# Unread TensorE products in half step 13 and inside the dt product of half step 22 of a Mamba block with a feed-forward tail

## The chip, the core and the metric

The kernel runs on one core of one Trainium2 chip. The metric is the device time of one execution in microseconds (us); less is better. The core's engines run side by side and meet at semaphores only: TensorE (PE; its weight loads are listed as PEld), VectorE (DVE), ScalarE (ACT), GpSimd (POOL) and SyncE (SP, which issues most of the DMAs). TensorE has two clock levels here, 1.2 and 2.4 GHz; the profile gives the granted clock as a share of the upper one, 0.50 or 1.00.

## What is computed

x has the shape 2 x 2048 x 256. All is float32. Cut to what matters:

```python
# both parts: x = x + layernorm(part(layernorm(x)))
def mamba(x):                                  # d_inner 512, state 16, conv width 4
    h = x * rsqrt(mean(x * x) + EPS) * norm_w
    u, z = split(h @ in_proj_w.T)
    uc = silu(conv_b + sum(pad(u)[k:] * conv_w[:, k] for k in range(4)))
    dt, B, C = split(uc @ x_proj_w.T)
    dt = softplus(dt @ dt_proj_w.T + dt_proj_b)          # the dt product
    h_t = exp(dt * A) * h_prev + dt * B * uc             # one scan per state
    y = sum_n(C * h_t) + uc * D
    return (y * silu(z)) @ out_proj_w.T + x
def ffn(x):                                    # hidden 1024, ternary weights
    h = silu(x @ w1.T * s1) * (x @ w2.T * s2)
    h = gelu(h @ h1.T * sh1)
    h = gelu(h @ h2.T * sh2)
    return h @ w3.T * s3
```

## The kernel before

The 4096 tokens are cut into 16 chunks of 256. The program is written by hand for each engine, with semaphores, and is cut in the same way on all of them: `body(c, par, ...)` is called once for each chunk c and runs through 32 half steps (`hs` 0 to 31), two for each of the 16 states. In the body of chunk c four pieces of work are interleaved: the scan of chunk c itself, the head of chunk c+1 (norm, in_proj, convolution, x_proj, dt product), the tail of chunk c-1 (the Mamba output, w1, w2 and h1 of the feed-forward part) and the end of chunk c-2 (h2, w3 and the last norm). Chunks 2 to 13 stand in a loop over pairs; bodies 2 to 14 have all four pieces, and the body of chunk 15 has no head.

The order on an engine is the order in which the code is written. On TensorE it is, within a half step: `turn` (four transposes of 128x128 that turn half of the scan's result S of the state before, L753), the piece of `end_step`, the piece of `tail_step`, the piece of `head_step`. An engine waits at a semaphore with all that stands behind it.

The pieces that matter here, by half step of the body:
- hs 10 to 13: the head's four in_proj products, L717, out `hP`. The two of hs 12 and 13 wait for ACT's copies of z out of `hP` (L1210), since they write over the same banks. ACT's copies of u (L1214) and the convolution follow.
- hs 14: `last_product` (w3), 32 products in L857 and L858, reading `Ghi` and `Glo`.
- hs 15 and 16: the first two quarters of w1 (`branch`, L729 and L730), each after the hs's turn. POOL's product `S<-X,Bs` (L567) of a later state needs the slot of S that the turn frees; ACT's `load_B` (L1160) in hs 16 waits for that product's step (L570), and behind it on ACT stand `dA` (L1134) and the copies of w1's results (L1298), which the next w1 products wait for.
- hs 22: two transposes of `xdbl` (L785), then the dt product in two halves, L793 (q = 0 and q = 1, two products each); the second waits for ACT's copy of `CT` (L1233).
- hs 24 to 31: the h1 layer, one tile of 16 products in each half step (L729, L730, in `Ghi`, `Glo` and `w_h`).

`keep_warm` (L796 to L801) makes products whose result nobody reads: ident by ident, 128x128, into a PSUM bank of the ring `fP` before its next use, after waiting for the bank's last reader. Before the change it is called in hs 22 and in hs 23 of the tail, six products each; in the profile one such product is two MATMUL records.

Of the kernel before, what the change touches and what calls it, by code (L numbers as in the profile page):

```python
# [25 lines left out]
P = 128  # L26
# [26 lines left out]
def build(nc, x, in_proj, x_proj, dt_proj, out_proj, w1, w2, h1, h2, w3, cols, w3_s, out):  # L53
# [22 lines left out]
    with ctx:  # L76
# [24 lines left out]
        ident = sb("ident", [P, P])  # L101
# [606 lines left out]
        def _(pe):  # L708
# [45 lines left out]
                                      ident[:, :])  # L754
                mm.then_inc(turn_pe.sem, 1)

            def head_step(h, hp, hs):
                if hs == 8:
                    pe.wait_ge(head_act.sem, head_act.at(h, "hn"))
                    pe.wait_ge(head_vec.sem, head_vec.at(h - 1, "delta"))  # L760
                    for k in range(KM):
                        for t in range(TT):
                            mm = pe.transpose(hP[0][:, k, t * P:(t + 1) * P], hn[:, t, k * P:(k + 1) * P],
                                              ident[:, :])
                    mm.then_inc(head_pe.sem, 1)
                if 10 <= hs < 14:
                    q = hs - 10
                    if q == 0:
                        pe.wait_ge(head_act.sem, head_act.at(h, "hT"))
                    elif q >= 2:  # L770

                        pe.wait_ge(head_act.sem, head_act.at(h, ("z0", "z1")[q - 2]))
                    for d in range(2):
                        m = (2 * q + d + DT) % (2 * DT)
                        mm = products(hP[(q + 1) % 2][:, d, :], lambda k: w_in[:, k, m * P:(m + 1) * P],
                                      lambda k: hT[:, k, :], KM)
                    mm.then_inc(head_pe.sem, 1)
                if hs == 20:
                    pe.wait_ge(head_act.sem, head_act.at(h, "silu1"))
                    products(hP[1][0:XC, 0, :], lambda k: w_x[:, k, :], lambda k: uc[hp][:, k, :],  # L780
                             DT).then_inc(head_pe.sem, 1)
                if hs == 22:
                    pe.wait_ge(head_act.sem, head_act.at(h, "dtx"))
                    for t in range(TT):
                        mm = pe.transpose(hP[1][:, 1, t * XC:(t + 1) * XC], xdbl[:, t * P:(t + 1) * P],  # L785
                                          ident[0:XC, 0:XC])
                    mm.then_inc(head_pe.sem, 1)
                    for q in range(2):
                        if q == 1:
                            pe.wait_ge(head_act.sem, head_act.at(h, "ct"))  # L790
                        for d in range(2):
                            m = 2 * q + d
                            mm = pe.matmul(hP[q][:, d, :], w_dt[:, m * P:(m + 1) * P], dtx, start=True, stop=True)  # L793
                        mm.then_inc(head_pe.sem, 1)

            def keep_warm(f, fp, count):  # L796

                steps, chunk, name = last_reader(f + 1, "h1_0")
                pe.wait_ge(steps.sem, steps.at(chunk, name))
                for _ in range(count):  # L800
                    pe.matmul(ring(1 - fp, "h1_0")[:, 0, 0:P], ident[:, :], ident[:, :], start=True, stop=True)  # L801

            def branch(f, fp, which, i, stream):

# [64 lines left out]
            def tail_step(f, fp, hs):  # L869
                if hs == 2:  # L870
                    for i in range(2):
                        steps, chunk, name = last_reader(f + 1, f"yT{i}")
                        pe.wait_ge(steps.sem, steps.at(chunk, name))
                        for t in range(TT):
                            pe.wait_ge(acc_vec.sem, acc_vec.at(f, f"y{t}_{N - 1}"))
                            for d in range(2):
                                mm = pe.transpose(ring(1 - fp, f"yT{i}")[:, d, t * P:(t + 1) * P],
                                                  acc[:, t, (2 * i + d) * P:(2 * i + d + 1) * P], ident[:, :])
                        mm.then_inc(tail_pe.sem, 1)
                if hs == 3:  # L880
                    pe.wait_ge(tail_vec.sem, tail_vec.at(f, "yz1"))
                    steps, chunk, name = last_reader(f + 1, "out")
                    pe.wait_ge(steps.sem, steps.at(chunk, name))
                    for t in range(TT):
                        mm = products(ring(1 - fp, "out")[:, t, :], lambda k: z[fp][:, k, t * P:(t + 1) * P],
                                      lambda k: w_out[:, k, :], DT)
                    mm.then_inc(tail_pe.sem, 1)
                if hs == 12:
                    pe.wait_ge(tail_act.sem, tail_act.at(f, "xf"))
                    steps, chunk, name = last_reader(f + 1, "xfT")  # L890
                    pe.wait_ge(steps.sem, steps.at(chunk, name))
                    for k in range(KM):
                        for t in range(TT):
                            mm = pe.transpose(ring(1 - fp, "xfT")[:, k, t * P:(t + 1) * P],
                                              o[:, t, k * P:(k + 1) * P], ident[:, :])
                    mm.then_inc(tail_pe.sem, 1)
                parts = {15: (0, (0, 1)), 16: (0, (2, 3)), 17: (1, B_ORDER[:2]), 20: (1, B_ORDER[2:])}
                if hs in parts:
                    which, some = parts[hs]
                    with pe.If(some_lo[0] != 0):  # L900
                        for i in some:
                            branch(f, fp, which, i, True)
                    with pe.Else():
                        for i in some:
                            branch(f, fp, which, i, False)
                if hs in (22, 23):
                    keep_warm(f, fp, 6)
                if 24 <= hs < (HALVES - 2 if is_last(f) else HALVES):
                    some = (hs - 24,)
                    with pe.If(some_lo[0] != 0):  # L910
                        for m in some:
                            hidden1(f, fp, m, True)
                    with pe.Else():
                        for m in some:
                            hidden1(f, fp, m, False)

            def end_step(g, gp, hs, tail):
                if 3 <= hs < 11:
                    with pe.If(some_lo[0] != 0):
                        hidden2(g, gp, hs - 3, True, tail)  # L920
                    with pe.Else():
                        hidden2(g, gp, hs - 3, False, tail)
                if hs == 14:
                    with pe.If(some_lo[0] != 0):
                        last_product(g, gp, True, tail)
                    with pe.Else():
                        last_product(g, gp, False, tail)

            def body(c, par, scan=False, head=False, tail=False, end=False, prepare=False,
                     seq_start=None, head_seq_start=None, j=None):  # L930
                for hs in range(HALVES):
                    n = hs // 2

                    if scan and n > 0:
                        turn(c, par, n - 1, hs % 2)
                    if tail and n == 0:
                        turn(c - 1, 1 - par, N - 1, hs % 2)
                    if tail and hs == 3:
                        tail_step(c - 1, 1 - par, hs)
                    if end:  # L940
                        end_step(c - 2, par, hs, tail)
                    if tail and hs != 3:
                        tail_step(c - 1, 1 - par, hs)
                    if head:
                        head_step(c + 1, 1 - par, hs)
                    if prepare and hs == HALVES - 1:
                        pe.wait_ge(late_in, 16 * LATE)
                    for s in stages_at(c, hs - 1):

                        pe.wait_ge(stage_marked, s + 1)  # L950
                        for i in range(2):
                            mm = pe.matmul(counts, ones[:, :], staging[s % 3][:, i * 2 * T:(i + 1) * 2 * T],
                                           start=(s == 0 and i == 0), stop=(s == len(STAGES) - 1 and i == 1))
                        mm.then_inc(stage_counted, 1)
                    if isinstance(c, int) and c == 1 and hs == 0:
                        pe.wait_ge(flag_set, 2)
                        some_lo[0] = pe.value_load(some_inexact[0:1, 0:1], min_val=0, max_val=1)
# [779 lines left out]
```

## Time and profile before

| | |
|---|---|
| median of 3 runs | 1749.94 us (1748.34 to 1750.32) |
| profiled execution, its own time | 1749.25 us |
| its span, first to last instruction | 1747.1 us |
| mean granted TensorE clock | 0.908 |
| busy share: PE, PEld, DVE, ACT, POOL | 81, 71, 76, 70, 65% |

The steady part is chunks 2 to 15; one chunk takes about 100 us. No engine is busy all the time, and which one is last changes within the chunk. So the busy shares say little: each stretch is read for the wait that ends last. In a row of the timeline the brackets give the idle time of the engine before the instruction and what ended it. In this document a "turn" names the four transposes L753 that open a half step on TensorE.

### The profile page before, as it was taken

The page shows a single profiled execution, that of the slowest core. Times are in us where ns is not written, and L with a number is a line of the kernel's source. Part 1 is how long each engine was busy: PE and PEld are TensorE (multiplying, and loading weights), DVE is VectorE, ACT ScalarE, POOL GpSimd, SP SyncE. Part 2 cuts the span into 40 slices and gives each one's busy share as a digit, 9 for nine tenths or more (in the row PEclk, how much of TensorE's full clock was granted, in tenths as well). Part 3 has the DMA queues.
Part 4 walks back from the last instruction along what each step waited for, and adds up shares of the span by engine and source line. Part 5 has one row for each costly group of instructions (what it writes and reads, how often), then busy time and mean ns, then how long its engine had stood idle before and what let it go on. Part 6 is the DMA issues. An engine that isn't in the chain of part 4 may idle for free.

```text
span 1747.1 us, 30661 instructions
## 1 busy us (share of the span) xinstructions
PE 1419.7 (81%) x9440; PEld 1247.3 (71%) x9440; DVE 1322.9 (76%) x1993; ACT 1219.5 (70%) x2641; POOL 1129.6 (65%) x1347
## 2 busy tenths in 40 slices
PE   4566688888888878889877888888878888888798
PEld 2122477788777867878776877777777887877698
DVE  2676887787768878687877878687877878788753
ACT  4445476877767786787768687677858778677653
POOL 1533657676676766677676766778766866867721
PEclk8788699989989988999889998999988899899899
DMA  3322100110101010010101011010100101010100
GB/s 109 110 85 85 36 26 20 35 36 20 40 27 38 26 38 28 20 45 20 45 22 38 27 23 43 20 45 26 39 21 26 44 21 38 26 32 29 30 3 15
DMA packets 38952, 63.78 MB, mean 37 GB/s; under 512 B 5233, under 2 KB 19441, under 8 KB 38657
## 3 DMA queue, kind: packets, MB, share of 16 engines
q10 hardware_dynamic: 18944, 33.83, 6.2%
q1 hardware_dynamic: 19712, 26.02, 4.7%
q8 instruction: 185, 3.03, 0.7%
q14 instruction: 111, 0.90, 0.2%
HBM read 55.38 MB, written 4.46 MB: 34 GB/s over the span
## 4 chain that ended last, share of the span: by engine, by line
POOL 24%; PE 23%; issue 20%; ACT 17%; DVE 13%; ACTq 1%; POOLq 1%; DVEq 0%; DMA 0%; SPq 0%
POOL S L567 16%; DVE S L1482 5%; PE fP L729 4%; ACT dA L1134 4%; PE sT L753 4%; PE fP L730 4%; PE hP L717 3%; DVE acc L1496 3%; ACT Rw L1330 2%; PE fP L857 1%; PE fP L858 1%; DVE hP L1511 1%; POOL S L570 1%; ACT L1330 1%; POOL Glo L637 1%
## 5 line engine op out<-in xcount | busy, mean ns | idle before, releaser
L567 POOL TENSOR_TENSOR S<-X,Bs 128x1024 f32<-128x1024 f32 x256 | 612.1, 2391 | 351.4 <-PE sT L753 249.2
L1482 DVE TENSOR_TENSOR_SCAN S<-dA,S 128x512 f32<-128x512 f32 x512 | 620.8, 1214 | 160.5 <-POOL S L570 87.0
L1134 ACT ACTIVATE dA<-delta,A 128x255 f32<-128x255 f32 x1024 | 446.2, 469 | 375.5 <-DVE S L1482 228.1
L729 PE MATMUL fP<-Ghi,w_h 128*128 128x256 f32 x1856 | 473.8, 294 | 41.0 <-DVE o L1556 21.4
L730 PE MATMUL fP<-Glo,w_h 128*128 128x256 f32 x1856 | 450.8, 282 | 0.0
L1496 DVE SCALAR_TENSOR_TENSOR acc<-sT,CT,acc 128x512 f32<-128x512 f32 x480 | 350.5, 733 | 99.0 <-PE sT L753 98.6
L753 PE MATMUL sT<-ident,S 128*128 128x128 f32 x2048 | 334.3, 292 | 89.1 <-DVE acc L1496 74.2
L729 PEld LDWEIGHTS fP<-Ghi,w_h 128*128 128x128 f32 x1856 | 353.7, 191 | 53.7 <-DVE o L1556 24.8
L753 PEld LDWEIGHTS sT<-ident,S 128*128 128x128 f32 x2048 | 253.1, 149 | 150.1 <-DVE acc L1496 75.4
L730 PEld LDWEIGHTS fP<-Glo,w_h 128*128 128x128 f32 x1856 | 354.2, 191 | 0.4
L637 POOL TENSOR_TENSOR Glo<-Rw,Ghi 128x1024 fp32r<-128x1024 f32 x86 | 202.7, 2357 | 58.3 <-ACT Ghi L1336 44.3
L729 PE MATMUL fP<-xf_hi,w 128*128 128x256 f32 x480 | 137.7, 319 | 51.4 <-ACT Rw L1298 39.8
L717 PE MATMUL hP<-e_sp,w_in 128*128 128x256 f32 x512 | 135.6, 413 | 30.5 <-ACT z L1210 28.6
L729 PEld LDWEIGHTS fP<-xf_hi,w 128*128 128x128 f32 x480 | 103.1, 215 | 58.8 <-ACT Rw L1298 43.3
L717 PEld LDWEIGHTS hP<-e_sp,w_in 128*128 128x128 f32 x512 | 100.7, 207 | 48.5 <-ACT z L1210 32.0
L1324 ACT ACTIVATE Rw<-fP,col 128x256 f32<-128x256 f32 x230 | 105.8, 460 | 42.1 <-PE fP L730 42.0
L730 PE MATMUL fP<-xf_lo,w 128*128 128x256 f32 x480 | 131.1, 305 | 0.0
L1511 DVE SCALAR_TENSOR_TENSOR hP<-u_ext,col,hP 128x256 f32<-128x256 f32 x192 | 79.4, 481 | 35.4 <-ACT hP L1220 34.1
L730 PEld LDWEIGHTS fP<-xf_lo,w 128*128 128x128 f32 x480 | 103.3, 215 | 0.0
L717 PE MATMUL fP<-w_out,z 128*128 128x256 f32 x240 | 78.6, 499 | 26.0 <-DVE z L1551 26.0
L717 PEld LDWEIGHTS fP<-w_out,z 128*128 128x128 f32 x240 | 60.5, 258 | 42.9 <-DVE z L1551 30.7
L570 POOL TENSOR_TENSOR S<-S,carried 128x4 f32<-128x4 f32 x256 | 56.9, 222 | 20.1
(212 smaller groups left out, 2226.4 us busy)
## 6 DMA issues: line engine op xcount, KB each, us to landing
Bs<-b_rows ACTq DMA_DIRECT2D x128, 256.0 KB, 3.1
Rw<-in_h SPq DMA_DIRECT2D x11, 512.0 KB, 3.2
xh<-in_x SPq DMA_DIRECT2D x16, 256.0 KB, 3.5
xt<-in_x SPq DMA_DIRECT2D x16, 256.0 KB, 3.8
out<-x SPq DMA_DIRECT2D x15, 256.0 KB, 2.8
x<-in_h SPq DMA_DIRECT2D x5, 512.0 KB, 3.2
Rw<-in_w SPq DMA_DIRECT2D x4, 512.0 KB, 6.2
w_in<-in_in_proj SPq DMA_DIRECT2D x1, 1024.0 KB, 5.7
```

The costliest lines, as they stand in the source:

```text
L567: pool.tensor_tensor(s[:, :, :], X[par][:, :, :], row[:, None, :].broadcast_to([P, DT, T]), ALU.mult).then_inc(scan_pool.sem, 1)
L570: pool.tensor_tensor(s[:, :, 0], s[:, :, 0], carried[:, n, :], ALU.add).then_inc(scan_pool.sem, 1)
L637: return pool.tensor_tensor(Glo[:, rows, :], Rw[:, rows, :], Ghi[:, rows, :].bitcast(F32), ALU.subtract)
L717: mm = pe.matmul(dst, lhs(i), rhs(i), start=(i == 0), stop=(i == k - 1))
L729: pe.matmul(dst, w[:, i, cols_], hi[:, i, :], start=(j == 0), stop=False)
L730: mm = pe.matmul(dst, w[:, i, cols_], lo[:, i, :], start=False, stop=(j == last))
L753: mm = pe.transpose(sT[t][:, d * P:(d + 1) * P], S[slot(par, n)][:, d, t * P:(t + 1) * P], ident[:, :])
L1134: a = act.activation(dA[half][:, i, 1:], delta[par][:, d, 1:], ACT.Exp, scale=A[:, d * N + n:d * N + n + 1])
L1324: act.activation(Rw[:, m, :], bank[:, 0, :], ACT.Copy, scale=scale).then_inc(steps.sem, 1)
L1482: a = dve.tensor_tensor_scan(pair, dA[half][:, :, :].rearrange("p d t -> p (d t)"), pair, 0.0, ALU.mult, ALU.add)
L1496: a = dve.scalar_tensor_tensor(y, sT[t][:, :], w, y, ALU.mult, ALU.add)
L1511: a = dve.scalar_tensor_tensor(u, u_ext[:, d, k:k + T], c_("conv_w", d * CONV + k), u, ALU.mult, ALU.add)
```

## The change

Two more places call `keep_warm`, whose arguments now name the bank of the ring by its use. In half step 13 ten products go to the bank that `last_product` writes in half step 14 (use `w3`); `end_step` stands ahead of `head_step`, so they come after the turn and before the in_proj product of that half step. It is made in the 14 bodies 2 to 15. In half step 22 eight products stand between the halves of the dt product, ahead of the wait for `ct`, in the 14 bodies 1 to 14. Those in half steps 22 and 23 stay.

```diff
-            def head_step(h, hp, hs):
+            def head_step(h, hp, hs, tail):
...
                     for q in range(2):
                         if q == 1:
+                            if tail:
+                                keep_warm(1 - hp, h - 1, "h1_0", 8)
                             pe.wait_ge(head_act.sem, head_act.at(h, "ct"))
...
-            def keep_warm(f, fp, count):
+            def keep_warm(par, chunk, use, count):
 
-                steps, chunk, name = last_reader(f + 1, "h1_0")
-                pe.wait_ge(steps.sem, steps.at(chunk, name))
+                steps, c, name = last_reader(chunk, use)
+                pe.wait_ge(steps.sem, steps.at(c, name))
                 for _ in range(count):
-                    pe.matmul(ring(1 - fp, "h1_0")[:, 0, 0:P], ident[:, :], ident[:, :], start=True, stop=True)
+                    pe.matmul(ring(par, use)[:, 0, 0:P], ident[:, :], ident[:, :], start=True, stop=True)
...
                 if hs in (22, 23):
-                    keep_warm(f, fp, 6)
+                    keep_warm(1 - fp, f + 1, "h1_0", 6)
...
             def end_step(g, gp, hs, tail):
+                if hs == 13 and tail:
+                    keep_warm(gp, g + 2, "w3", 10)
```

Half steps 12 and 13 on TensorE in the loop's body of an even chunk, before: the turn of hs 12, the tail's transposes of `o`, the in_proj product, the turn of hs 13, the next in_proj product, and the turn of hs 14.

```order
L753 MATMUL sT0<-ident,S0 128x128 x4
L889 ISA
L891 ISA
L894 MATMUL fP0<-ident,o 128x128 x4
L772 REGISTER_ALU
L717 MATMUL hP1<-e_sp,w_in 128x256 x4
L753 MATMUL sT1<-ident,S0 128x128 x4
L772 REGISTER_ALU
L717 MATMUL hP0<-e_sp,w_in 128x256 x4
L747 REGISTER_ALU
L749 REGISTER_ALU
L753 MATMUL sT0<-ident,S1 128x128 x4
```

The same place with the change:

```order
L717 MATMUL hP1<-e_sp,w_in 128x256 x4
L753 MATMUL sT1<-ident,S0 128x128 x4
L801 REGISTER_ALU
L803 MATMUL fP1<-ident 128x128 x10
L772 REGISTER_ALU
L717 MATMUL hP0<-e_sp,w_in 128x256 x4
L747 REGISTER_ALU
L749 REGISTER_ALU
L753 MATMUL sT0<-ident,S1 128x128 x4
```

The ten products stand ahead of the second in_proj product and of all that follows it.

Half step 22 on TensorE in the same body, before, from the products of `keep_warm` to those of half step 23:

```order
L801 MATMUL fP0<-ident 128x128 x6
L783 REGISTER_ALU
L785 MATMUL hP1<-ident,xdbl 128x112 x2
L793 MATMUL hP0<-xdbl,w_dt 128x256 x2
L790 REGISTER_ALU
L793 MATMUL hP1<-xdbl,w_dt 128x256 x2
L753 MATMUL sT1<-ident,S2 128x128 x4
L801 MATMUL fP0<-ident 128x128 x6
```

The same place with the change:

```order
L803 MATMUL fP0<-ident 128x128 x6
L783 REGISTER_ALU
L785 MATMUL hP1<-ident,xdbl 128x112 x2
L795 MATMUL hP0<-xdbl,w_dt 128x256 x2
L803 MATMUL fP0<-ident 128x128 x8
L792 REGISTER_ALU
L795 MATMUL hP1<-xdbl,w_dt 128x256 x2
L753 MATMUL sT1<-ident,S2 128x128 x4
L803 MATMUL fP0<-ident 128x128 x6
```

The eight products stand between the halves of the dt product; nothing else changes its place.

## Rows read from the trace of the kernel before

**Rows 1.** The page's chain that ended last: shares of the span by engine.
```profile
POOL 24%; PE 23%; issue 20%; ACT 17%; DVE 13%; ACTq 1%; POOLq 1%; DVEq 0%; DMA 0%; SPq 0%
```

**Rows 2.** Timeline of PE, chunk 6, hs 12 to 16: start, duration, [idle before].
```profile
721.95 1.99 PE L717 MATMUL hP<-e_sp,w_in 128*128 128x256 f32 x8 [1.85 <-ACT z L1210]
723.78 0.60 PE L753 MATMUL sT<-ident,S 128*128 128x128 f32 x4
724.26 1.99 PE L717 MATMUL hP<-e_sp,w_in 128*128 128x256 f32 x8
726.09 0.60 PE L753 MATMUL sT<-ident,S 128*128 128x128 f32 x4
...
730.32 0.60 PE L753 MATMUL sT<-ident,S 128*128 128x128 f32 x4
...
735.92 0.38 PE L729 MATMUL fP<-xf_hi,w 128*128 128x256 f32 x1 [2.68 <-ACT Rw L1298]
```

**Rows 3.** Timelines of POOL and of ACT behind the turn of hs 15, chunk 6.
```profile
731.09 2.39 POOL L567 TENSOR_TENSOR S<-X,Bs 128x1024 f32<-128x1024 f32 x1 [2.27 <-PE sT L753]
...
734.24 0.87 ACT L1134 ACTIVATE dA<-delta,A 128x255 f32<-128x255 f32 x2 [3.03 <-POOL S L570]
```

**Rows 4.** Timeline of PE, chunk 5: in_proj product of hs 12, turn of hs 14.
```profile
615.91 2.42 PE L717 MATMUL hP<-e_sp,w_in 128*128 128x256 f32 x8 [2.29 <-ACT z L1210]
...
621.59 0.60 PE L753 MATMUL sT<-ident,S 128*128 128x128 f32 x4
```

**Rows 5.** What PE waited for, whole run: idle us in total, times, longest us.
```profile
PE fP L729 <- ACT Rw L1298: 39.8, 15, 2.7
PE hP L717 <- ACT z L1210: 28.6, 13, 2.3
```

**Rows 6.** Timeline of PE, chunk 6, hs 22 to 24, and the turn of hs 29.
```profile
750.12 0.65 PE L753 MATMUL sT<-ident,S 128*128 128x128 f32 x4 [1.65 <-DVE acc L1496]
...
752.63 1.13 PE L793 MATMUL hP<-xdbl,w_dt 16*128 16x256 f32 x4
754.76 1.12 PE L793 MATMUL hP<-xdbl,w_dt 16*128 16x256 f32 x4 [1.01 <-ACT CT L1233]
...
756.31 1.50 PE L801 MATMUL fP<-ident 128*128 128x128 f32 x12
757.65 0.60 PE L753 MATMUL sT<-ident,S 128*128 128x128 f32 x4
...
771.40 0.66 PE L753 MATMUL sT<-ident,S 128*128 128x128 f32 x4 [0.97 <-DVE acc L1496]
```

**Rows 7.** Timeline of PE, chunk 7: turn of hs 22, products of hs 23, turn of hs 29.
```profile
847.97 0.66 PE L753 MATMUL sT<-ident,S 128*128 128x128 f32 x4 [1.28 <-DVE acc L1496]
...
855.34 2.77 PE L801 MATMUL fP<-ident 128*128 128x128 f32 x12
...
870.33 0.60 PE L753 MATMUL sT<-ident,S 128*128 128x128 f32 x4
```

**Rows 8.** Timeline of PE, chunk 5: turns of hs 22 and of hs 29.
```profile
646.02 0.66 PE L753 MATMUL sT<-ident,S 128*128 128x128 f32 x4 [1.65 <-DVE acc L1496]
...
667.29 0.66 PE L753 MATMUL sT<-ident,S 128*128 128x128 f32 x4 [0.40 <-DVE acc L1496]
```

**Rows 9.** Busy time by stretch: length, engines' busy us (x), granted clock, DMA share, GB/s.
```profile
351.10:357.92 6.82, 6.82 (x29) 5.98 (x29) 3.95 (x6) 5.83 (x16) 5.80 (x5) 0.50 0.03 7
...
1358.03:1364.86 6.83, 6.83 (x28) 5.99 (x28) 3.91 (x5) 5.86 (x16) 5.84 (x5) 0.50 0.01 2
651.47:654.88 3.41, 3.41 (x16) 2.96 (x15) 2.83 (x3) 3.06 (x10) 3.33 (x4) 0.50 0.00 1
```

**Rows 10.** Timeline of PE, chunk 15 (without a head), hs 14.
```profile
1614.54 0.63 PE L753 MATMUL sT<-ident,S 128*128 128x128 f32 x4 [1.21 <-DVE acc L1496]
1617.42 0.58 PE L857 MATMUL fP<-w,Ghi 128*128 128x256 f32 x1 [2.25 <-POOL Glo L637]
```

**Rows 11.** PE alone by stretch, chunks 2 to 15: length, busy (x), granted clock, DMA.
```profile
282.83:1640.00 1357.17, 1142.72 (x7917) 0.92 0.10 31
```

More of the change, by code:

```diff
@@ L944, in body @@
                     if head:
-                        head_step(c + 1, 1 - par, hs)
+                        head_step(c + 1, 1 - par, hs, tail)
                     if prepare and hs == HALVES - 1:
```

## The prediction

> **What bounds the kernel now.** I read the page's chain first. It is spread over POOL, PE, ACT and DVE [rows 1], so no engine bounds the whole; a product that nobody reads costs nothing where PE would wait anyway, and its full length where PE is last. The question is which of the two holds at the two new places, and what the lower clock level costs there. So I read PE's timeline next, in the steady bodies, with the bracket in front of each group.
>
> Half steps 12 to 15: PE waits for ACT's first copy of z, 1.85 us in chunk 6, and starts the in_proj product of hs 12 at 721.95. From there no bracket stands on PE up to the turn of hs 15 at 730.32, 8.4 us later [rows 2]. POOL's product of S has then waited 2.27 us for that turn, ACT 3.03 us for POOL, and PE itself 2.68 us for ACT's copies of w1 [rows 2, 3]. That is a closed ring, PE, POOL, ACT, PE, in which every engine but PE waited, so PE's stretch from hs 12 to the turn of hs 15 is on the path. It is so in all 13 bodies that have a head and an end (2 to 14): the wait for z comes 13 times, 28.6 us together, and the one for the w1 copies 15 times, 39.8 us, with a longest of 2.7, thus nearly the same length each time [rows 5].
>
> Half steps 22 to 29: PE is idle for 1.01 us between the halves of the dt product [rows 6]. Behind it PE has no wait for some half steps, and at hs 29 the turn waits for DVE, by 0.97 us in chunk 6, where hs 23 ran at the upper level, and still by 0.40 us in chunk 5, where a spell of 3.41 us at the lower level lay over it [rows 6, 8, 9]. From the turn of hs 22 to the turn of hs 29 it is 21.28 us in chunk 6 (750.12 to 771.40) and 21.27 in chunk 5 (646.02 to 667.29): the short spell costs nothing. In chunk 7, where the lower level held for 6.8 us, it is 22.36 us (847.97 to 870.33) and the turn waits for nothing: 1.08 us lost [rows 7]. Four chunks have such a long spell in hs 22 to 24 (2, 7, 9 and 12; the first and the last of them in rows 9).
>
> **Half step 13: ten products.** Two records make one product. In hs 23 of chunk 6, 12 records stand from 756.31 to the next turn at 757.65, 1.34 us or 0.112 us each [rows 6]; 20 records are 2.24 us. They stand behind the turn of hs 13 and ahead of the in_proj product of the same half step, in the middle of the stretch without a wait. Their own wait, for ACT's last h2 copy, ends before hs 12 on ACT, ahead of the z copy that PE already waits for, so it adds nothing. What is queued behind them is the second u half for ACT's copy and the convolution, w3, and the turn of hs 15, on which POOL waits. Nothing covers them: 13 x 2.24 = 29.1 us. The low bound is zero, if something unseen absorbs them; I take 2.24, since in rows 2 and 3 all three others wait.
>
> Do they keep the clock up? A spell lies over hs 12 to 14 in chunk 5: from the start of the hs 12 product to the turn of hs 14 it is 5.68 us, against 4.14 in chunk 6 [rows 4, 2]. The clock fell there after the 2.29 us in which PE waited for z, ahead of the new products. The other idle stretch nearby, 2.68 us ahead of the w1 products of hs 16 [rows 2], begins more than 8 us behind them. They fill neither, and I give them no gain.
>
> In the body of chunk 15 there is no head, and PE idles 1.21 us ahead of the turn of hs 14 and 2.25 us behind it, for POOL [rows 10]. The 2.24 us go in there and cost nothing. A milder clock behind them could give up to 1 us; I take 0.
>
> **Half step 22: eight products.** 16 x 0.112 = 1.79 us, of which 1.01 us is the idle time that they replace: PE's next work comes 0.78 us later. In a chunk at the upper level the 0.97 us at hs 29 covers this, so 0; without that cover it would be 0.8 x 14 = 11 us. ACT works on the two halves one after the other, in hs 23 and hs 24, so it needs the second a half step later than the first and doesn't wait for it. The gain is the clock. With the idle time gone PE goes on without a pause from the first half to hs 23, and I expect the fall that now follows this pause to stay away. Where the spell was short, nothing is gained (the row of chunk 5 above); where it was long, 1.08 us each: 4 x 1.08 = 4.3 us. The bounds are 0 and, if the eight too run at the lower level (2.77/12 = 0.231 each, 3.7 us for 16, 2.7 beyond the idle time, less 0.4 to 1.0 of cover), a loss of about 2 us a chunk. I take the gain, since chunk 6 runs through here at the upper level even with the pause in [rows 6], so little is missing.
>
> **The sum.** 29.1 - 4.3 + 0 = +24.8 us. On the profiled execution's own 1749.25 us that is 1774; the median of the runs is 0.7 us above it, so 1774.5 there. I put down 1774.
>
> The trace has 0.112 us for one record of 128 columns. The Trainium skill, "TensorE: Matmul & The Clock Gate", section "Back-to-back issue gap", gives about 81 ns for each product of 128 columns in a sustained stream. By that figure ten products in two records each would take an estimated 1.6 us, and the sum would be about +17 us. The trace does not agree, so its row is used.
>
> **The rivals.** (a) The clock stays up from hs 12 on: the added stream reaches the spells of hs 12 and of hs 16 after all. The one of hs 12 costs 1.54 us where it occurs (5.68 - 4.14); if half of the 13 chunks have one there now and half have a like one over hs 16, 13 x 1.54 = 20 us come back (an estimate), and the time is 1754. Against it is where the idle stretches lie, before and well behind the ten.
>
> (b) Faster than before: the ring of a chunk gets longer, the falls come at other places, and nearly all time at the lower level moves off PE's stretches on the path. From 283 to 1640 us the mean clock is 0.92 [rows 11], so 2 x 0.08 x 1357 = 217 us run at the lower level and PE loses half of that, 108 us, over all stretches, on the path or not. It decides from 24.8 us: a good fifth of the loss would have to go, beyond what I counted. At 34 us gone the time is 1741. Nothing in the rows says that the new places are that lucky.
>
> (c) The same shift the other way: one spell more on the path in half of the chunks, 7 x 1.54 = 11 us, 1785.
>
> (d) The eight of hs 22 don't hold the clock, and run at the lower level in about half of the bodies: 7 x 2 us, and the gain of 4.3 us is not there: 1774 + 14 + 4 = 1792.
>
> (e) The change does not do what it says: the ten are hidden, because the ring is released by something else (POOL's load of rows, say). Then only hs 22 is left, 1745 to 1750. Rows 3 speak against it, in which POOL is idle for 2.27 us ahead of the turn.
>
> **How the numbers follow.** The sum as it stands 0.72; (a) 0.08; (b) 0.03; (c) 0.09; (d) 0.05; (e) 0.03. The sum's own spread, by the spells that a longer chunk moves, is some 9 us to either side. From 1760 to 1787 it holds nearly all of the first case and of (c), 0.8 in all; (a), (b), (d) and (e) are left out. A measurement of this kernel tells about 0.2%, 3.5 us, from no change. Faster by more than that: (b) and half of (e), 0.04; within it: the other half of (e), 0.02; slower: 0.94.
>
> **What would show it.** Right: in the profile after, the turn of hs 13 to that of hs 14 takes 2.2 us longer in chunks 2 to 14 (2.31 us now in chunk 6), PE has no bracket from the hs 12 product to the turn of hs 15, and POOL's wait ahead of its product of S is longer by as much; PE's wait for the w1 copies stays at 2.7 us. In hs 22 the wait for `CT` is gone, the granted clock over hs 22 to 24 is 1.00 in nearly all chunks, and the turn of hs 22 to the turn of hs 29 is 21.3 us everywhere, with a wait for DVE of some 0.2 us. A chunk takes about 2 us more. Wrong: the ten are followed by a new wait ahead of the turn of hs 14 or 15 (then something else is last), the spells at hs 12 and 16 vanish (rival a), or hs 22 still has them (rival d). The sum would be wrong without any of this if the spells at the chunk's border, in hs 31 to 3, change by more than 1 us a chunk.

## The result, and the profile after

| | before | after |
|---|---|---|
| median | 1749.75 us | 1775.35 us (1768.83 to 1777.13, 4 runs) |
| ratio to before, 95% interval | | 1.0141 [1.0113, 1.0168] |
| span of the profiled execution | 1747.1 us | 1774.6 us |
| mean granted clock | 0.908 | 0.925 |

The change makes the kernel 1.4% slower, although it raises the mean clock of TensorE. The forecast was 1774 us.

Where the added time lies is read from the starts of the turns. The table adds up each piece of the body over chunks 2 to 14, from the turn of one half step to that of another (each worked out from the two timelines of TensorE; 32 and 34 are hs 0 and 2 of the next body):

| half steps | before, us | after, us | difference |
|---|---|---|---|
| 2 to 4 | 156.4 | 151.4 | -5.0 |
| 4 to 12 | 311.0 | 318.4 | +7.4 |
| 12 to 13 | 69.6 | 71.2 | +1.6 |
| **13 to 14** | 35.6 | 59.2 | **+23.6** |
| 14 to 15 | 55.0 | 54.9 | 0.0 |
| 15 to 17 | 108.0 | 112.7 | +4.7 |
| 17 to 22 | 151.4 | 147.7 | -3.7 |
| **22 to 29** | 280.7 | 276.6 | **-4.0** |
| 29 to 34 | 134.6 | 135.3 | +0.7 |
| chunks 2 to 14 | | | +25.2 |
| up to the turn of hs 2 of chunk 2 | 279.5 | 281.4 | +1.9 |

The first reading is the timeline of TensorE in chunk 6, hs 12 to 16, of the kernel after, which answers to [rows 2] (start, duration, what, [idle before <-releaser]):

```profile
731.13 1.99 PE L717 MATMUL hP<-e_sp,w_in 128*128 128x256 f32 x8 [2.13 <-ACT z L1214]
732.97 0.60 PE L753 MATMUL sT<-ident,S 128*128 128x128 f32 x4
733.40 2.40 PE L803 MATMUL fP<-ident 128*128 128x128 f32 x20
735.63 1.89 PE L717 MATMUL hP<-e_sp,w_in 128*128 128x256 f32 x8
737.36 0.60 PE L753 MATMUL sT<-ident,S 128*128 128x128 f32 x4
...
741.59 0.60 PE L753 MATMUL sT<-ident,S 128*128 128x128 f32 x4
...
747.17 0.38 PE L729 MATMUL fP<-xf_hi,w 128*128 128x256 f32 x1 [2.67 <-ACT Rw L1302]
```

No bracket stands between 731.13 and the turn of hs 15 at 741.59, as before, and the stretch has grown from 8.37 to 10.46 us. The turn of hs 13 to that of hs 14 takes 4.39 us (732.97 to 737.36) instead of 2.31. Then POOL and ACT in the same chunk, which answer to [rows 3]:

```profile
742.35 2.38 POOL L567 TENSOR_TENSOR S<-X,Bs 128x1024 f32<-128x1024 f32 x1 [4.39 <-PE sT L753]
```

```profile
745.49 0.87 ACT L1138 ACTIVATE dA<-delta,A 128x255 f32<-128x255 f32 x2 [3.02 <-POOL S L570]
```

POOL waits 4.39 us for the turn instead of 2.27, the 2.1 us that TensorE spends on the ten products; ACT's wait for POOL and TensorE's wait for ACT (2.67 us) have not changed. The delay goes once around the ring. It is so in every chunk: POOL's wait for this turn is 2.20 to 3.86 us in chunks 2 to 14 before and 4.32 to 6.09 us after, 39.0 and 65.2 us together, 26.2 us more. VectorE's wait for the turn of hs 14 grows too, from 0.44 to 2.52 us in chunk 6. Over the whole run the waits of TensorE answer to [rows 5] (idle us in total, times, longest us):

```profile
PE fP L729 <- ACT Rw L1302: 40.2, 15, 3.0
PE hP L717 <- ACT z L1214: 27.6, 13, 2.3
```

The page's group of POOL's product of S, before and after (busy us, mean ns | idle us before them <-releaser of most of it):

```profile
L567 POOL TENSOR_TENSOR S<-X,Bs 128x1024 f32<-128x1024 f32 x256 | 612.1, 2391 | 351.4 <-PE sT L753 249.2
L567 POOL TENSOR_TENSOR S<-X,Bs 128x1024 f32<-128x1024 f32 x256 | 610.8, 2386 | 378.9 <-PE sT L753 308.0
```

All of its idle time is 27.5 us more (351.4 to 378.9), as much as the span. The part put down to the turns grows by 58.8 us, more than the change can add: the part put down to ACT's `carry` is 28.7 us less (76.5 to 47.8), so some waits only changed their last releaser. VectorE's waits for the turns grow from 98.6 to 129.0 us.

Half step 22, TensorE in chunk 7, the chunk of [rows 7]:

```profile
861.39 0.66 PE L753 MATMUL sT<-ident,S 128*128 128x128 f32 x4 [1.64 <-DVE acc L1500]
...
863.90 1.13 PE L795 MATMUL hP<-xdbl,w_dt 16*128 16x256 f32 x4
...
866.94 1.13 PE L795 MATMUL hP<-xdbl,w_dt 16*128 16x256 f32 x4
...
882.68 0.66 PE L753 MATMUL sT<-ident,S 128*128 128x128 f32 x4 [0.96 <-DVE acc L1500]
```

The pause for `CT` is gone, the halves of the dt product stand 3.04 us apart instead of 2.13 (both in chunk 7), and the turn of hs 22 to that of hs 29 is 21.29 us instead of 22.36. The granted clock over this place answers to [rows 9] (stretch, length, busy us (x), granted clock, DMA share, GB/s):

```profile
351.00:362.00 11.00, 9.75 (x71) 1.00 0.32 100
861.00:872.00 11.00, 10.48 (x77) 1.00 0.25 82
```

No chunk from 2 to 14 has a spell at the lower level in half steps 22 and 23 any more.

### The profile page after: what moved, and what is told of

Read it like the earlier page. It is cut to its first block, busy times and chain, and to the rows that moved or that the text cites. A ratio compares the mean times of both kernels' runs of the same rounds, so it can differ in the third digit from the quotient of the medians.

```text
span 1774.6 us, 31681 instructions
## 1 busy us (share of the span) xinstructions
PE 1444.7 (81%) x9944; PEld 1285.4 (72%) x9944; DVE 1325.9 (75%) x1993; ACT 1219.2 (69%) x2641; POOL 1128.4 (64%) x1347
## 4 chain that ended last, share of the span: by engine, by line
POOL 24%; PE 22%; issue 20%; ACT 17%; DVE 14%; ACTq 1%; POOLq 1%; DVEq 0%; DMA 0%; SPq 0%
POOL S L567 15%; DVE S L1486 6%; ACT dA L1138 4%; PE fP L729 4%; PE hP L717 3%; PE fP L730 3%; DVE acc L1500 3%; PE sT L753 3%; ACT Rw L1334 2%; PE fP L803 2%; PE fP L859 2%; PE fP L860 2%; ACT L1334 1%; ACT o L1170 1%; POOL S L570 1%
## 5 line engine op out<-in xcount | busy, mean ns | idle before, releaser
L567 POOL TENSOR_TENSOR S<-X,Bs 128x1024 f32<-128x1024 f32 x256 | 610.8, 2386 | 378.9 <-PE sT L753 308.0
L729 PE MATMUL fP<-Ghi,w_h 128*128 128x256 f32 x1856 | 481.3, 297 | 43.7 <-DVE o L1560 25.2
L730 PE MATMUL fP<-Glo,w_h 128*128 128x256 f32 x1856 | 458.3, 285 | 0.0
L1500 DVE SCALAR_TENSOR_TENSOR acc<-sT,CT,acc 128x512 f32<-128x512 f32 x480 | 351.0, 734 | 129.9 <-PE sT L753 129.0
L753 PE MATMUL sT<-ident,S 128*128 128x128 f32 x2048 | 329.1, 288 | 99.7 <-DVE acc L1500 85.5
L729 PEld LDWEIGHTS fP<-Ghi,w_h 128*128 128x128 f32 x1856 | 359.0, 193 | 55.6 <-DVE o L1560 28.8
L730 PEld LDWEIGHTS fP<-Glo,w_h 128*128 128x128 f32 x1856 | 359.9, 194 | 0.4
L803 PE MATMUL fP<-ident 128*128 128x128 f32 x864 | 110.0, 280 | 2.5 <-ACT Rw L1328 0.7
L803 PEld LDWEIGHTS fP<-ident 128*128 128x128 f32 x864 | 102.1, 194 | 10.9 <-DVE Rw L1573 5.3
L717 PE MATMUL fP<-w_out,z 128*128 128x256 f32 x240 | 65.4, 433 | 26.5 <-DVE z L1555 26.5
```

The costliest lines, as they stand in the source:

```text
L567: pool.tensor_tensor(s[:, :, :], X[par][:, :, :], row[:, None, :].broadcast_to([P, DT, T]), ALU.mult).then_inc(scan_pool.sem, 1)
L717: mm = pe.matmul(dst, lhs(i), rhs(i), start=(i == 0), stop=(i == k - 1))
L729: pe.matmul(dst, w[:, i, cols_], hi[:, i, :], start=(j == 0), stop=False)
L730: mm = pe.matmul(dst, w[:, i, cols_], lo[:, i, :], start=False, stop=(j == last))
L753: mm = pe.transpose(sT[t][:, d * P:(d + 1) * P], S[slot(par, n)][:, d, t * P:(t + 1) * P], ident[:, :])
L803: pe.matmul(ring(par, use)[:, 0, 0:P], ident[:, :], ident[:, :], start=True, stop=True)
```

## Experiments

All kernels are compared with the kernel before, run beside them on the same chip; its medians there were 1751.9, 1751.5 and 1747.0 us in the three groups, so the ratios say more than the medians. The pieces and the spells are read from one profiled execution of each kernel. They differ between executions without any edit: the kernel before alone lies between 1745.2 and 1763.0 us in its 48 executions of these groups, with a mean clock of 0.912 to 0.894.

| kernel | unread products in hs | median, us | ratio to before [95%] |
|---|---|---|---|
| the change | 13, 22 (8), 22 and 23 (6) | 1775.4 | 1.0141 [1.0113, 1.0168] |
| e1_only13 | 13, 22 and 23 (6) | 1775.6 | 1.0166 [1.0131, 1.0201] |
| e2_only22 | 22 (8), 22 and 23 (6) | 1746.6 | 0.9971 [0.9957, 0.9986] |
| e3_13x20 | twenty in 13, 22 and 23 (6) | 1803.2 | 1.0297 [1.0278, 1.0317] |
| e4_fill12 | 12, 22 and 23 (6) | 1741.6 | 0.9940 [0.9926, 0.9954] |
| e8_12_22 | 12, 22 (8), 22 and 23 (6) | 1739.7 | 0.9936 [0.9920, 0.9952] |
| e6_12_16_22 | 12, 16, 22 (8), 22 and 23 (6) | 1737.1 | 0.9920 [0.9903, 0.9936] |
| e5_fill16 | 16, 22 and 23 (6) | 1751.4 | 0.9993 [0.9977, 1.0009] |
| e7_no_warm | nowhere | 1743.4 | 0.9952 [0.9935, 0.9969] |
| e9_12_no_old | 12 | 1741.7 | 0.9956 [0.9931, 0.9980] |
| e10_13_no_old | 13 | 1776.2 | 1.0162 [1.0141, 1.0183] |

**One half of the change alone: half step 13.**

```diff
                         if q == 1:
-                            if tail:
-                                keep_warm(1 - hp, h - 1, "h1_0", 8)
```

> The change's half step 13 alone; half step 22 as before. Theory A (the ten products stand bare on TensorE's stretch from hs 12 to the turn of hs 15): the turn of hs 13 to that of hs 14 is 2.1 us longer in each of bodies 2 to 14, 27 us in all, and since the long spells in hs 22 may come back, the time is about 1778 (1772 to 1784), the mean clock below that of the full change. Rival B (the slowdown comes from low-clock spells that the other chunk length moves): the time lies anywhere between 1750 and 1785 and the sum over the half steps outside hs 13 carries it. Rival C (the products of hs 22 cost the time): about 1750.

It has the whole slowdown. Hs 13 to 14 is 22.8 us longer in sum than before, 4.40 us in eleven of the thirteen chunks. The clock rival falls: all other pieces of chunks 2 to 14 together are 3.4 us shorter than before. What I had not expected is hs 22 to 29: without the eight products it is also 4.2 us shorter than before. TensorE in chunk 7 of this kernel:

```profile
859.11 0.66 PE L753 MATMUL sT<-ident,S 128*128 128x128 f32 x4 [1.65 <-DVE acc L1498]
861.62 1.12 PE L793 MATMUL hP<-xdbl,w_dt 16*128 16x256 f32 x4
863.76 1.12 PE L793 MATMUL hP<-xdbl,w_dt 16*128 16x256 f32 x4 [1.01 <-ACT CT L1235]
...
880.40 0.66 PE L753 MATMUL sT<-ident,S 128*128 128x128 f32 x4 [0.41 <-DVE acc L1498]
```

and the granted clock behind it:

```profile
865.82:869.24 3.42, 3.42 (x18) 0.50 0.02 5
```

Pause and spell are both there, but the spell is a short one, and TensorE still arrives 0.41 us ahead of DVE at hs 29: 21.29 us from turn to turn. Eleven of the chunks 2 to 14 have such a short spell in this kernel and none has a long one. So the long spells can go without the eight products. That the longer chunk took them away is my reading and not shown: e3, whose chunk is longer still, has long ones in chunks 3, 6 and 13.

**The other half alone: half step 22.**

```diff
-                if hs == 13 and tail:
-                    keep_warm(gp, g + 2, "w3", 10)
```

> The change's half step 22 alone. Theory A: the wait for CT between the halves of the dt product and the spells over hs 22 to 24 are gone, hs 22 to hs 29 takes 21.3 us in all chunks, 4 us less in all; the time is about 1746 (1742 to 1750). Rival C (the eight products cost): 14 x 0.8 us, about 1761. Rival B: the shorter chunk moves spells elsewhere, and the gain is changed by up to 5 us to either side though hs 22 to 29 is the same.

0.29% faster, with an interval that leaves no change out. Hs 22 to 29 is 3.5 us shorter, as expected. In hs 17 to 21 there are 11.7 us more, with eight spells that now lie in hs 20 instead of three, and 7.4 us less in hs 21 to 22: the wait for DVE ahead of the turn of hs 22 takes most of these up. The eight products gain nearly what was priced at their place, when they are alone; they don't cost.

**Twice as many products in half step 13.**

```diff
-                    keep_warm(gp, g + 2, "w3", 10)
+                    keep_warm(gp, g + 2, "w3", 20)
```

(and hs 22 as before)

> Twenty products in half step 13 instead of ten, half step 22 as before. Theory A: the length is linear, hs 13 to hs 14 is 4.2 us longer than before in 13 bodies, 54 us, and the time about 1804 (1798 to 1811). Theory A would be wrong, and a wait that limits the cost right, if it were under 1790. Rival B: the time is not ordered by the number of products.

The time is nearly linear in the products: 1751.9, 1775.6 and 1803.2 us with none, ten and twenty in hs 13, all in one group of runs. TensorE in chunk 2:

```profile
323.71 0.60 PE L753 MATMUL sT<-ident,S 128*128 128x128 f32 x4
324.15 4.63 PE L801 MATMUL fP<-ident 128*128 128x128 f32 x40
328.61 1.89 PE L717 MATMUL hP<-e_sp,w_in 128*128 128x256 f32 x8
330.34 0.60 PE L753 MATMUL sT<-ident,S 128*128 128x128 f32 x4
```

From turn to turn it is 6.63 us. With none it is 2.32, with ten 4.40: the first ten cost 2.08 us and the next ten 2.23, which is 20 x 0.112. The ten themselves take 2.23 us both times. Once there are any, what stands around them is 0.15 us shorter (in chunk 6, from start to start: 2.31 us before are 0.48 + 1.83, and in the kernel after 0.43 + 2.23 + 1.73); why is not known.

**The same ten, one half step earlier.** They stand in the head's piece of hs 12, ahead of the wait for ACT's copy of z, in bodies 2 to 14; those of hs 13 and the eight of hs 22 are out. Only the lines added in `head_step`:

```diff
                     elif q >= 2:
 
+                        if q == 2 and end:
+                            keep_warm(1 - hp, h - 1, "w3", 10)
                         pe.wait_ge(head_act.sem, head_act.at(h, ("z0", "z1")[q - 2]))
```

> Ten unread products in half step 12 ahead of the wait for ACT's copy of z, where TensorE idles for 2.3 us, in bodies 2 to 14; none in 13, hs 22 as before. Theory A: 20 records of 0.104 to 0.112 us are 2.1 to 2.2 us and fit into the idle time, so they cost nothing; the low-clock spell that falls over hs 12 to 14 in six chunks (1.5 us each) is gone; about 1741 (1736 to 1748). Rival D (any more products in this ring cost their length, wherever they stand): about 1777. Rival B: the spells come back in hs 16, 1745 to 1755.

This is the run that separates place from number: the same products in the same 13 bodies, and 34 us less than e1. TensorE in chunk 6:

```profile
719.10 0.60 PE L753 MATMUL sT<-ident,S 128*128 128x128 f32 x4
719.54 0.60 PE L896 MATMUL fP<-ident,o 128*128 128x128 f32 x4
719.97 2.40 PE L803 MATMUL fP<-ident 128*128 128x128 f32 x20
722.27 1.99 PE L717 MATMUL hP<-e_sp,w_in 128*128 128x256 f32 x8
...
724.11 0.60 PE L753 MATMUL sT<-ident,S 128*128 128x128 f32 x4
724.59 1.99 PE L717 MATMUL hP<-e_sp,w_in 128*128 128x256 f32 x8
726.42 0.60 PE L753 MATMUL sT<-ident,S 128*128 128x128 f32 x4
```

They fill the wait for z and end with it, and POOL's wait for the turn of hs 15 in chunk 6 is what it was before:

```profile
731.41 2.38 POOL L567 TENSOR_TENSOR S<-X,Bs 128x1024 f32<-128x1024 f32 x1 [2.27 <-PE sT L753]
```

No spell is left over hs 12 to 14: hs 12 to 13 and 13 to 14 are together 8.8 us shorter than before, and the turn of hs 13 to that of hs 14 is 2.32 us in every chunk.

**Half steps 12 and 22, and 12, 16 and 22.** The ten of hs 16 stand ahead of its turn, in the bank that the turn writes, where TensorE waits for ACT's copies of w1.

```diff
-            def turn(c, par, n, t):
+            def turn(c, par, n, t, fill=0):
...
+                for _ in range(fill):
+                    pe.matmul(sT[t][:, 0:P], ident[:, :], ident[:, :], start=True, stop=True)
                 for d in range(DT):
...
-                        turn(c, par, n - 1, hs % 2)
+                        turn(c, par, n - 1, hs % 2, 10 if end and hs == 16 else 0)
```

> The ten products in half step 12 ahead of the wait for z, and the eight of half step 22; none in 13. Theory A (each place is worth what it is worth alone): 1741 less 4, about 1737 (1733 to 1743). Rival E (the places share one gain, since moving the chunk's length already takes the long spells out of hs 22): no better than the one of hs 12 alone, 1740 to 1744.

> As the one with half steps 12 and 22, and ten more products in half step 16 ahead of the turn, where TensorE waits 2.7 us for ACT's copies of w1. Theory A: no low-clock spell over hs 12 to 14, 16 to 17 or 22 to 24 is left, 13 x some 0.7 us less again, about 1728 (1722 to 1736). Rival D (the delayed turn of hs 16 holds DVE up): VectorE's adding in hs 17 comes 2.2 us later and the ring pays for it, 1745 to 1765.

> The ten products of half step 16 alone, hs 22 and 23 as before. Theory A: the spells over hs 16 and 17 are gone, about 9 us less, 1741 (1735 to 1748). Rival D: the turn of hs 16 is 2.2 us late for VectorE, and the time is 1755 to 1775.

In hs 12 and 22 together the ratio is 0.9936, and 0.9940 with hs 12 alone: the intervals overlap, and whether hs 22 adds anything there stays open (the two were in different groups of runs). Hs 16 does to its own place what was expected and little to the time: I had put down 1741 us for e5 and 1728 for e6, and both missed their ranges with 1751.4 and 1737.1. TensorE in chunk 7 of e5:

```profile
832.58 2.39 PE L753 MATMUL sT<-ident 128*128 128x128 f32 x20
834.81 0.60 PE L755 MATMUL sT<-ident,S 128*128 128x128 f32 x4
835.86 0.39 PE L729 MATMUL fP<-xf_hi,w 128*128 128x256 f32 x1 [0.45 <-ACT Rw L1300]
...
842.61 0.66 PE L755 MATMUL sT<-ident,S 128*128 128x128 f32 x4 [1.12 <-DVE acc L1498]
844.47 0.38 PE L729 MATMUL fP<-xf_hi,w 128*128 128x256 f32 x1 [1.20 <-DVE Rw L1571]
```

Of the idle 2.68 us 0.45 are left, the spells over hs 16 are gone, and hs 15 to 17 is 9.5 us shorter over the chunks. But hs 17 to 22 is 10.1 us longer. The clock now falls in hs 20, behind the two waits for DVE at its start, in 11 chunks instead of 3:

```profile
845.33:848.74 3.41, 3.41 (x16) 0.54 0.01 4
```

The saved time is given back one place further on, in the execution that was profiled; it was the slowest of ten (1757.1 us, of 1746.7 to 1757.1). With hs 12 and 22 filled as well (e6) there are eight spells in hs 20 and none in hs 12, 16 and 22, and the kernel is the fastest of all, 0.8% under the one before; whether by hs 16 or by the others can't be told from 0.9920 and 0.9936.

**No unread products at all.** The old ones of hs 22 and 23 are taken out too; then the same with the ten of hs 12, and with the ten of hs 13.

```diff
-                if hs in (22, 23):
-                    keep_warm(1 - fp, f + 1, "h1_0", 6)
```

> No unread products at all, those of half steps 22 and 23 gone too. Theory A (they stand where TensorE waits for POOL's low part, and hold the clock for the h1 layer behind): the spells in hs 22 to 24 become longer and reach the first h1 tiles, 1 to 2 us in each of 14 chunks, 1765 (1755 to 1778). Rival F (they are in the way of the turn of hs 24 as much as they help): 1745 to 1755.

> The ten products in half step 12 ahead of the wait for z, and no others (those of hs 22 and 23 taken out). Theory A (the place in hs 12 is worth what it is worth alone): the spells over hs 12 to 14 that the kernel without any unread product still has are gone, 4 spells of 1.5 us: 1743 less 6, about 1737 (1732 to 1742). Rival E (the gains of the two changes are the same chunk-length effect and do not add): 1742 to 1746.

> The ten products in half step 13, and no others (those of hs 22 and 23 taken out). It differs from the one with the ten in half step 12 by a place of one half step on TensorE. Theory A: the cost of hs 13 does not depend on the others; 27 us above the kernel without any, less up to 4 for spells: about 1768 (1763 to 1773), and some 30 us above the one with half step 12. Rival B (the clock decides): the two lie within 10 us of each other.

My theory on the old ones falls: without them the kernel is 0.5% faster than before, not slower (1743.4 us, where I had put down 1765). The lower level does lie over hs 22 to 24 in all of the chunks 2 to 14, nearly always for two or three times as long as a short spell (chunk 7 three times), but TensorE has less to do there, and the turn of hs 29 comes no later. TensorE in chunk 7:

```profile
844.23 0.66 PE L753 MATMUL sT<-ident,S 128*128 128x128 f32 x4 [1.65 <-DVE acc L1494]
846.25 0.63 PE L785 MATMUL hP<-ident,xdbl 112*128 112x112 f32 x2 [1.37 <-ACT xdbl L1225]
846.82 4.13 PE L793 MATMUL hP<-xdbl,w_dt 16*128 16x256 f32 x8
...
865.54 0.62 PE L753 MATMUL sT<-ident,S 128*128 128x128 f32 x4
```

That is 21.31 us from the turn of hs 22 to that of hs 29. In this chunk TensorE has no wait left at hs 29, and comes only 0.02 to 0.04 us later than the 21.27 to 21.29 us of the chunks in which the turn waits for DVE. The mean clock of this kernel is 0.888, below that of the kernel before (0.908), and it is faster.

Hs 12 on top of it gives nothing that can be measured (0.9956 against 0.9952), so the gains of e4 and e7 do not add; why is not settled. With the ten in hs 13 (e10) it is 34 us slower than with the ten in hs 12, where I had expected some 30. Against the kernel without any (e7) it is 33 us slower by the medians and some 37 us by the ratios (1.0162 and 0.9952), where I had expected up to 27, and its 1776.2 us miss the range that ended at 1773. Of it hs 13 to 14 has 25.8 us and hs 15 to 17 another 11 us, with spells over hs 16 in all thirteen chunks instead of eight.

What hs 22 to 29 takes in each trace (us, sum over chunks 2 to 14, time at the lower level in brackets):

| kernels | unread products in hs 22 and 23 | hs 22 to 29 |
|---|---|---|
| before, e1, e3, e4, e5 | the old twelve | 280.7 (44.4), 276.5 (37.5), 280.3 (44.4), 279.6 (41.0), 281.9 (44.4) |
| after, e2, e8, e6 | twelve and the new eight | 276.6 (0), 277.1 (3.4), 276.7 (0), 274.6 (0) |
| e7, e9, e10 | none | 276.7 (102.4), 276.4 (92.2), 276.8 (105.8) |

The eight do take the spells away, and taking the old twelve out gives the same time, with more than twice as much time at the lower level as before.

## Why the prediction was right, point by point

**TensorE is last from hs 12 to the turn of hs 15.** Right. It rested on three waits that follow each other [rows 2, 3] and on their being equal in every chunk [rows 5]. In the kernel after, POOL's wait for the turn has grown by 2.12 us in chunk 6 and the two waits behind it have not; e4 shows that the same products cost nothing a half step earlier. The waits are not as equal as the prediction took them: POOL's before is 2.20 to 2.29 us in seven chunks and 3.84 to 3.86 in the six that have a spell in hs 12.

**The ten products, 13 x 2.24 = 29.1 us.** Right in kind, a little large. At the upper level they cost 2.08 us a chunk, 27.0 in all; 23.6 were measured from hs 13 to 14, since before 5.5 us of spells lay in that piece (35.6 less 13 x 2.32) and after 2.0. The step that was mis-sized is the length of the first ten, which counted the records alone and left out the 0.15 us that are saved around them; e3 has the 2.23 us for the next ten. By the figure of about 81 ns of the Trainium skill ("TensorE: Matmul & The Clock Gate", section "Back-to-back issue gap") they would be an estimated 1.6 us; the traces have 2.1 to 2.2.

**No gain for the clock at hs 12 and 16.** Right: the kernel after has as many spells at these places as before (in chunks 2 to 14, 5 that begin in hs 12 and 11 in hs 16, against 6 and 9). The idle time lies ahead of the products. e4, which puts them into it, has no spell over hs 12 to 14.

**The body of chunk 15: nothing.** Right: from the turn of hs 12 to that of hs 15 it is 15.3 us in both.

**Half step 22, -4.3 us.** The size was right, -4.0 us, and the reason only half. The eight products do hold the clock up: e1 has 11 spells that begin in hs 22 or 23 of chunks 2 to 14, the kernel after none. But the 4 us need no eight products: e1 has them too, with short spells that the wait at hs 29 pays, and so has e7, without the old twelve and with longer ones. Where the step failed is in adding the two halves as if one did not bear on the other: alone the eight give 3.5 us at their place (e2), and on top of the ten of hs 13 nothing there (276.6 us against 276.5 in e1). In the whole time it stays open: the medians are alike (1775.4 and 1775.6), the ratios 1.0141 and 1.0166 with intervals that overlap. The cover was mis-sized too: the turn of hs 29 was to keep a wait of some 0.2 us, and it keeps 0.94 to 0.97 in all 13 chunks. The 0.9 us by which the turn of hs 24 comes later in chunk 6 (8.44 us behind the turn of hs 22, 7.54 before) are gone by the turn of hs 28 (17.86 and 17.84).

**What was left out.** The other pieces of the body were taken as unchanged; they are from -5.0 to +7.4 us, and +5.7 in sum. The spells moved: the time at the lower level goes from 73.7 to 47.8 us in hs 2 to 4, from 10.2 to 41.0 in hs 4 to 12, from 24.4 to 33.9 in hs 15 to 17 and from 23.4 to 7.1 in hs 17 to 22, each time the way in which the piece changed. The range had 9 us to either side for them. That the forecast of 24.8 us lies so close to the 25.6 measured by the medians is in part luck. Between the two profiled executions it is 27.5 us: 5.5 too much was put down for hs 13 (29.1 against 23.6) and 0.3 for hs 22, and 8.0 that stood at nought came on top, 5.7 in the other pieces, 1.9 ahead of them and 0.4 behind.

**The rivals.** (a) and (b) wanted the spells to vanish, which they did only in hs 22. (c) wanted 11 us more of spells on the path; the other pieces and the start have 7.6 us more, so it is half there, inside the range. (d) wanted the eight to run at the lower level; they ran at the upper one. (e) wanted the ten hidden in hs 13; POOL's wait grew by their length instead, and they are hidden only where e4 puts them.

## What to carry to other kernels

Before work that nobody reads is put into an engine's queue, look for the bracket: it is free where the engine idles for longer than it takes, and costs its full length where the engine has no wait up to the point on which others depend. Here a half step decided between +1.7% and -0.6% (e1 and e4). And a spell at the lower clock costs only where the engine is last; a kernel with a lower mean clock can be the faster one, so count the time between two points on the path, not the clock.

## What the runs showed of the hardware

Filling one idle stretch can move the fall of the clock to the next one: with hs 16 filled (e5), 11 chunks had a spell in hs 20 instead of 3, and 9.5 us gained came back as 10.1 us lost. And at a place that the edit did not touch, the spells of hs 22 and 23 were four long and five short ones before, eleven short ones with ten products in hs 13 (e1), and three long and six short ones with twenty (e3). Each count is of one execution. Single places can be priced from a trace; the places that the change did not touch moved by 5.7 us in sum here, on 1750.
